# First attention of a two-layer-deep attention block: two engines' head programs without a loop, and 41 extra fp32 matmuls ahead of the first head

## The reference

```python
q = _rope(proj(Wq, bq)); k = _rope(proj(Wk, bk)); v = proj(Wv, bv)   # 2 x 16 heads, 2048 tokens, 16 wide
scores = jnp.einsum('bhtd,bhsd->bhts', q, k) / scale                  # 2048 x 2048 of each head
attn = jax.nn.softmax(scores, axis=-1)
out = jnp.einsum('bhts,bhsd->bhtd', attn, v)
```

## Time and profile before

| | us |
|---|---|
| median of three executions | 3238.8 |
| lowest, highest | 3226.86, 3239.49 |
| profiled execution, its own time | 3247.33 |
| its span (first to last instruction) | 3245.5 |
| first attention in it | about 181 to 1634 |
| opening in it | 190.55 to 243.6 |

### The profile page before, as it was taken

The page is one execution under the profiler, slowest core; times in us unless marked ns, Lnnn a source line. Parts: engine busy times, 40 slices in busy tenths (PEclk is TensorE's granted clock), DMA queues, the critical chain, the costliest instruction groups (busy, mean ns, idle before and its releaser), DMA issues. The chain is left out here.

```text
span 3245.5 us, 63295 instructions
## 1 busy us (share of the span) xinstructions
PE 3022.2 (93%) x23672; PEld 1882.9 (58%) x23672; DVE 2484.3 (77%) x4820; ACT 2272.8 (70%) x4998; POOL 732.7 (23%) x1019
## 2 busy tenths in 40 slices
PE   8969999999999999999985999999999999999995
PEld 5733333333333333333354787878788787878784
DVE  4668899999989989989455767676767767677774
ACT  3407788888878888878864666666667666767673
POOL 3510000000000000000054343333334343434331
PEclk9957999999989999989997999999999999999998
DMA  3332222233222223322040000000000000000002
GB/s 111 114 82 39 35 30 39 41 41 41 41 40 38 37 29 41 41 41 40 12 166 17 1 1 0 0 0 0 0 1 35 1 1 0 0 0 0 0 1 70
DMA packets 47115, 99.37 MB, mean 31 GB/s; under 512 B 17184, under 2 KB 29472, under 8 KB 40480
## 3 DMA queue, kind: packets, MB, share of 16 engines
q1 hardware_dynamic: 42400, 95.48, 15.7%
q10 hardware_dynamic: 4544, 1.38, 0.2%
HBM read 71.13 MB, written 25.69 MB: 30 GB/s over the span
## 5 line engine op out<-in xcount | busy, mean ns | idle before, releaser
L691 DVE TENSOR_REDUCE mx<-aux 128x1 f32<-128x1024 f32 x1024 | 1246.5, 1224 | 122.3 <-PE aux L556 114.6
L661 ACT ACTIVATE probs<-scores 128x512 f32<-128x512 f32 x2048 | 1117.3, 597 | 258.0 <-PE scores L580 151.2
L556 PE MATMUL aux<-k_stack,q_stack 48*128 48x512 f32 x2048 | 795.3, 467 | 28.1 <-DMA k_stack<-qk_dram 20.0
L580 PE MATMUL scores<-q_stack,k_stack 50*128 50x512 f32 x2048 | 781.0, 458 | 13.2 <-ACT probs L661 13.2
L592 PE MATMUL pv<-probs,v_ones 128*32 128x256 f32 x8192 | 672.7, 401 | 0.1
L580 PEld LDWEIGHTS scores<-q_stack,k_stack 50*128 50x128 f32 x2048 | 318.7, 189 | 441.3 <-ACT probs L661 415.6
L592 PEld LDWEIGHTS pv<-probs,v_ones 128*32 128x32 f32 x8192 | 163.1, 109 | 374.8 <-ACT probs L661 271.7
L556 PEld LDWEIGHTS aux<-k_stack,q_stack 48*128 48x128 f32 x2048 | 321.9, 194 | 78.8 <-DVE mx L691 51.8
L1245 PE MATMUL bank<-QO,w_sb 128*128 128x128 f32 x2816 | 333.7, 278 | 0.9 <-ACT QO L1331 0.9
L1245 PEld LDWEIGHTS bank<-QO,w_sb 128*128 128x128 f32 x2816 | 321.5, 193 | 12.1 <-issue 10.3
L522 POOL CAST m_parts<-head_max 128x16 fp32r<-128x16 f32 x32 | 6.3, 196 | 1362.1 <-DVE head_max L696 1362.1
(11 more groups left out here) (176 smaller groups left out, 4565.6 us busy)
## 6 DMA issues: line engine op xcount, KB each, us to landing
q_stack<-qk_dram SPq DMA_DIRECT2D x192, 128.0 KB, 5.0
k_stack<-qk_dram SPq DMA_DIRECT2D x192, 128.0 KB, 7.1
qk_dram<-qkT_hi SPq DMA_DIRECT2D x32, 256.0 KB, 3.0
qk_dram<-qkT_lo SPq DMA_DIRECT2D x32, 256.0 KB, 3.6
out<-x_sb SPq DMA_DIRECT2D x9, 384.0 KB, 4.3
wqkv_sb<-in_wqkv SPq DMA_DIRECT2D x2, 1536.0 KB, 7.7
w_sb<-in_w SPq DMA_DIRECT2D x2, 1408.0 KB, 11.7
x_sb<-in_x SPq DMA_DIRECT2D x1, 2048.0 KB, 19.0
```

The costliest lines, as they stand in the source:

```text
L556: last = nc.tensor.matmul(aux[:, ring["unit"], block_of_keys % 2], q_stack[rows, r % BODY, tile * P:(tile + 1) * P], k_stack[rows, r % BOD ...
L580: nc.tensor.matmul(scores[:, item % BANKS1], k_stack[0:SCORE_ROWS, r % BODY, s * P:(s + 1) * P], q_stack[0:SCORE_ROWS, r % BODY, j * 512:( ...
L661: nc.scalar.activation(probs[:, item % PROBS], scores[:, item % BANKS1], ACT.Exp, scale=float(D1) ** -0.5).then_inc(probs_ready, 1)
L691: nc.vector.reduce_max(mx[:, slot, tile, half:half + 1], aux[:, unit].rearrange("p a k -> p (a k)"), AX.X).then_inc(max_taken, 1)
```

## The change

ACT and DVE get the ten rounds of `all_heads` written out, as PE has them; the lowering of semaphores at a round's end stays in all of them, and POOL and SP keep their loop. In the opening, PE gets a fp32 matmul behind every second maximum matmul, 41 in all. Its stationary operand is the identity, its moving operand 256 columns of `V1` (written in the stage before), and its result goes to a bank of `scores` that nobody reads before the first score overwrites it. It waits for nothing.

```diff
+            def keep_array_busy(bank):
+
+                nc.tensor.matmul(scores[:, bank, 0:TB * D1], ident[:], V1[:, 0].rearrange("p t d -> p (t d)"), start=True, stop=True)
+
             for m in range(AHEAD):
                 score_for_max(m // (BLOCKS * TB), m // BLOCKS % TB, m % BLOCKS)
+                if m % 2 == 1:
+                    keep_array_busy(m // 2 % BANKS1)
                 if m == 2 * FIRST_ROWS - 1:
                     maximum_rows(0)
...
-            all_heads(act, head, ((rows_in_psum, 1), (scores_ready, BLOCKS * TB), (pv_done, TB)))
+            all_heads(act, head, ((rows_in_psum, 1), (scores_ready, BLOCKS * TB), (pv_done, TB)), looped=False)
...
-            all_heads(dve, head, ((max_in_psum, DVE_ITEMS),))
+            all_heads(dve, head, ((max_in_psum, DVE_ITEMS),), looped=False)
```

## The result

The changed kernel takes 3277.6 us (median of four executions, 3273.57 to 3284.03) where the kernel before takes 3232.8 us (four, 3222.93 to 3239.49). The ratio is 1.0121 with a 95% interval of 1.0081 to 1.0161: it is 1.2% slower. The forecast was 3256.4 us, with a range up to 3267. The sign was the expected one, and so were the clock in the opening and the engine that bounds it; the size was not, because a cost on PE was left out.

What follows compares the result with a forecast made beforehand. DVE was taken to pace the opening, and PE to become its bound with the added matmuls at the lower clock. Terms of 0 + 17.6 + 0 us on the median 3238.8 us gave 3256.4 us, range 3229 to 3267 us.

Steps and rivals of the forecast that it cites:

- Written-out programs, 0 us: Round ends of the heads: ten branches fewer on ACT and DVE each, covered by PE's pause; 0 us, at most 13 plus 25.
- The attribution of the pause to PE's own fifteen falls: Round ends: PE's 1.30 us pause is filled by its fifteen semaphore falls of 0.15 us, not caused by ACT.
- The clock stays at 0.50 in the opening: Opening: with half whole-array and half 48-row matmuls, TensorE was taken to stay at its lower clock, costing 17.6 us.
- three busy stretches at the lower clock: Projections' start, first heads and opening: PE was busy without the clock rising, and part of the matmuls used few rows.
- 41 units at +0.43 us, 17.6 us: Opening at the lower clock: a unit grows from 1.28 to 1.71 us, with PE as the bound; 17.6 us in all.
- Weight loads hide there, as the even distances show: Output projection: weight loads hide beside its 128 x 256 fp32 matmuls, which take 0.86 us each at the lower clock.
- at most +20 us if weight loads show: Opening: upper bound on the added matmuls' cost if weight loads are not hidden, against the forecast +17.6 us.
- At the upper clock the matmul is hidden, a gain of 1.6 us: Opening: 0.86 us of PE work lies below DVE's 1.22 us, so a unit falls from 1.28 to some 1.24 us.
- 34 us at 0.50 behind the opening, as before: First heads behind the opening: the stretch at the lower clock was expected to stay unchanged, 34 us.
- The clock's luck behind the round ends: Heads: clock falls behind round ends are worth 0 to 25 us in an execution; 58 us were at 0.50 when profiled.
- I carry the difference over to the median unchanged: Whole kernel: the +17.6 us, summed against the profiled 3247.3 us, is added to the median 3238.8 us as it is.

## Why the prediction was wrong

- **Written-out programs, 0 us**: right. Alone they measure 0.9982 (0.9937 to 1.0028), and the ten pauses stand. The attribution of the pause to PE's own fifteen falls was right too, shown by taking them away.
- **The clock stays at 0.50 in the opening**: right, in the profiles of the change and of the matmuls alone. The reading that a busy PE is not enough, drawn from three busy stretches at the lower clock, was borne out by the openings with one and with four added matmuls, and best by the one with all its matmuls on 48 rows, which stayed at 0.50 for 70 us though its columns left no gap.
- **41 units at +0.43 us, 17.6 us, "Weight loads hide there, as the even distances show"**: this step failed. The added matmul's own columns were sized right, 0.86 us. But that they hide was read from a neighbourhood in which every matmul uses all 128 rows. The opening puts the added matmul between matmuls of 48 rows, and each change of rows exposes 0.29 us: 2 x 0.29 x 41 = 24 us, and 17.6 + 24 = 41.4 us against 41.3 measured. I allowed "at most +20 us if weight loads show", without working it out. That loads don't always hide could be seen in the trace before, though not how much it would be here: in the earlier trace rows the pattern at the lower clock has 2.16 us from one set of weightings to the next, while its columns are two pairs at 0.43 us each and one set of fp32 weightings of 256 columns, side by side, at the 0.86 us of the added matmul: 1.71 us. The starts divide the 0.45 us between the two:

```profile
273.77 0.79 PE L580 MATMUL scores<-q_stack,k_stack 50*128 50x512 f32 x1
273.78 0.79 PE L556 MATMUL aux<-k_stack,q_stack 48*128 48x512 f32 x1
274.37 0.62 PE L580 MATMUL scores<-q_stack,k_stack 50*128 50x512 f32 x1
274.37 0.63 PE L556 MATMUL aux<-k_stack,q_stack 48*128 48x512 f32 x1
```

From the first pair to the second are 0.60 us, 0.17 over its columns, with no change of rows; from there to the weightings at 274.92 are 0.55 us, 0.12 over; and from those to the next pair, by the sum, 1.01 us, 0.15 over. So 0.27 us lie at the two changes to 128 rows and back, less than the 0.58 us that the added matmul pays, and the rest between the pairs. I used the 2.16 us for the clock's price only, and did not ask what it was made of.
- **At the upper clock the matmul is hidden, a gain of 1.6 us**: not reached here, and it would not have held. With the twelve matmuls ahead, the two units that ran at it took 1.28 and 1.29 us, as long as a unit without the added matmul and more than the 1.24 forecast: in 0.66 + 0.63 us (181.52 to 182.18 to 182.81) the columns are 0.43 us each, and the changes of rows make it longer than DVE's 1.22 us.
- **34 us at 0.50 behind the opening, as before**: 31.1 us, right, and partly by luck: over the traces in which the opening ends at 0.50 and the heads follow at once, it was 11 us (the matmuls alone) to 49 us (the added matmuls in twos). The clock's luck behind the round ends, "0 to 25 us", was too low: the kernel with ACT and DVE written out had 106 us at 0.50 there, 46 us by the factor of 0.43, and the stretch behind the last round end alone can cost 40 us, as the kernels with twelve and with four matmuls showed.
- **The median, "I carry the difference over to the median unchanged"**: with the opening at +41.3 us the sum would have been 3238.8 + 41.3 = 3280.1 us, 2.5 us from the measured median. So close a match is partly luck, since the medians of the kernel before differ by up to 13 us from one session to the next (3232.8, 3238.8, 3245.7 us).

## What to carry to other kernels

Before a matmul is placed between others, ask whether it uses the same rows of the array as its neighbours, not only how many columns it has: here a change of rows cost 0.29 us at the lower clock and 0.23 us at the upper one, against 0.43 and 0.21 us for a 512-column fp32r matmul. Where a repeating pattern takes longer than its columns, find out what the rest is before using the period as a price. And look into a pause for the waiting engine's own sequencer records before believing the releaser named beside it; taking those records away was worth 1.3%, some 43 us. The ten pauses themselves were 13 of them; in the profiles 37 and 47 us went between the first score and the last, most of the rest of them because the clock no longer fell behind the pauses.

## What the runs showed of the hardware

- A PE that is busy all the time kept the lower clock for 94 us in the changed kernel (half of its columns on 48 rows) and for 70 us with every matmul on 48 rows and no gap between the columns, and got the upper one after 5 us with four whole-array matmuls for every pair of 48-row ones.
- The stretch of scores and weightings at the end of the heads kept either clock for its whole length: 429 matmuls in 52 us at 1.00, 419 in 90 us at 0.50. So a fall of the clock behind the last pause of 1.3 us, some 25 us ahead of it, can cost more than all ten pauses together.
- The falls of semaphores on PE cost 0.15 us each though a record shows 51 ns; the pause of 1.3 us went with them.
- A load hides beside a matmul on the same 48 rows, and doesn't where the rows go from 48 to 128 or back, whatever the type. Side by side on rows that don't overlap, two matmuls of the heads start within 0.01 us of each other, yet the next such pair starts 0.60 us later for 0.43 us of columns; what exposes the 0.17 us was not tried.
